# A four-layer graph network on one core: first-layer attention on two halves of the partitions, codes loaded behind the edge tables, look-ups two groups ahead

## The reference

```
feat = x @ W1 -> [N, 4 heads, 16]
e = leaky_relu(el[src] + er[dst]);  ee = exp(e - segment_max(e, dst)[dst])
alpha = ee / segment_sum(ee, dst)[dst]
h = elu(segment_sum(feat[src] * alpha, dst) + b1)        # 64 columns
second step: the same on h @ W2, one head, 128 columns
```

## Time and profile before

| | us |
|---|---|
| median of 3 runs | 2458.64 (2457.08 to 2461.86) |
| the profiled execution, its own time | 2458.36 |
| its span, first to last instruction | 2456.6 |
| prep and stage a, to the barrier | 0 to 537 |
| first softmax | 537 to 580 |
| stage b | 580 to 764 |
| stage c | 764 to 1051 |
| all that comes behind | 1051 to 2457 |

### The profile page before, as it was taken

One profiled execution on the slowest core, in us unless ns is written; L12 is line 12 of the kernel. 1 busy time (PEld: TensorE's weight loads), 2 busy tenths in 40 slices (PEclk: granted clock), 3 DMA queues, 4 the chain that ended last, 5 costly groups with the idle time before them and its releaser, 6 DMA issues.

```text
span 2456.6 us, 32122 instructions
## 1 busy us (share of the span) xinstructions
PE 1917.6 (78%) x7888; PEld 1280.3 (52%) x7888; DVE 1718.3 (70%) x6542; ACT 1120.3 (46%) x3061; POOL 1382.8 (56%) x1388
## 2 busy tenths in 40 slices
PE   2998988975877688847756665999995899969883
PEld 2988888864663223236645553666563222235552
DVE  5644444448775876579968986899895566678773
ACT  0322222214665566625535554566664555524332
POOL 5777777730003677700047773477665777727776
PEclk9766666655556788755558886999997555556655
DMA  5655555544224567624449775233531999923340
GB/s 152 191 155 155 155 156 155 155 156 173 105 109 150 171 184 205 183 81 146 151 133 258 212 208 161 93 130 129 166 121 54 335 367 315 305 72 104 127 139 28
DMA packets 272958, 401.94 MB, mean 164 GB/s; under 512 B 98472, under 2 KB 115009, under 8 KB 272645
## 3 DMA queue, kind: packets, MB, share of 16 engines
q1 hardware_dynamic: 215852, 310.35, 38.8%
q0 software_dynamic: 43904, 75.95, 11.7%
q10 hardware_dynamic: 13016, 13.59, 1.6%
HBM read 222.06 MB, written 185.39 MB: 166 GB/s over the span
## 4 chain that ended last, share of the span: by engine, by line
POOL 16%; DVE 13%; issue 11%; ACT 8%; PE 5%; DMA 2%; POOLq 0%; SPq 0%; DVEq 0%; ACTq 0%
POOL ring L667 8%; POOL big L667 4%; POOL out_dram L673 4%; DVE stats L683 3%; ACT outr L729 3%; DVE G L1161 3%; ACT big L1806 2%; DMA ring<-x_t,idx 1%; DVE mv L692 1%; DVE z L1533 1%; DVE z L1876 1%; PE bank L1549 1%; ACT big L1814 1%; PE bank L1545 1%; ACT hT L1792 1%
## 5 line engine op out<-in xcount | busy, mean ns | idle before, releaser
L729 ACT ACTIVATE outr<-z,rn 128x128 f32<-128x128 f32 x784 | 322.7, 483 | 297.1 <-DMA out_dram<-outr,idx 103.7
L667 POOL DMA_INDIRECT ring<-in_x_dram,idx x392 | 379.9, 969 | 137.3 <-issue 118.3
L667 POOL DMA_INDIRECT ring<-x_t,idx x280 | 266.9, 953 | 303.4 <-SPq L303 209.1
L667 POOL DMA_INDIRECT ring<-hidden_e,idx x196 | 195.5, 997 | 309.2 <-DVE idx L1415 251.6
L673 POOL DMA_INDIRECT x_t<-outr,idx x196 | 234.3, 1195 | 160.5 <-ACT outr L729 114.7
L1161 DVE TENSOR_TENSOR_SCAN G<-cont,G,bank 64x512 f32<-64x512 uint8 (+1 forms) x192 | 240.6, 1253 | 35.1 <-PE bank L1239 32.4
L673 POOL DMA_INDIRECT out_dram<-outr,idx x196 | 195.5, 997 | 102.5 <-issue 58.2
L1937 PE MATMUL bank<-DB,z 20*128 20x512 f32 x196 | 201.2, 1128 | 22.8 <-DVE outr L1391 8.1
L1239 PE MATMUL bank<-ident,msg 128*64 128x128 f32 (+1 forms) x588 | 153.2, 415 | 71.4 <-DVE msg L1146 68.5
L1033 DVE BATCH_NORM_STATS2 stats<-ring 128x6 f32<-128x128 f32 x196 | 42.7, 281 | 232.0 <-DMA ring<-in_x_dram,idx 231.8
L1549 PEld LDWEIGHTS bank<-W_s,G 65*128 65x128 f32 (+1 forms) x784 | 165.5, 311 | 65.7 <-issue 63.3
(11 more groups left out here) (384 smaller groups left out, 4548.4 us busy)
## 6 DMA issues: line engine op xcount, KB each, us to landing
hT<-in_x_dram SPq DMA_DIRECT2D x194, 256.0 KB
x_t<-outr SPq DMA_DIRECT2D x98, 256.0 KB
ring<-x_e SPq DMA_DIRECT2D x98, 256.0 KB
x_t<-xload SPq DMA_DIRECT2D x48, 512.0 KB, 3.2
xsrc_e<-ring SPq DMA_DIRECT2D x49, 256.0 KB, 2.8
xd_e<-ring ACTq DMA_DIRECT2D x49, 256.0 KB
ring<-xsrc_e SPq DMA_DIRECT2D x49, 256.0 KB
x_t<-xT SPq DMA_DIRECT2D x49, 256.0 KB
```

The costliest lines, as they stand in the source:

```text
L667: nc.gpsimd.indirect_dma_start(to(c), None, table, bass.IndirectOffsetOnAxis(ap=idx[:, kind, (g + 1) * GT + c:(g + 1) * GT + c + 1].bitcas ...
L729: ins = nc.scalar.activation(to[:, k, :], frm[:, k, :], ACT.Identity, bias=sc[:, k, 1:2], scale=sc[:, k, 0:1])
```

## The change

Stage b runs on two halves of the edges at once. The first 25 groups (`GA`, 12800 edges) lie on partitions 0 to 63, the other 24 (`GB`) on partitions 64 to 127. Step j handles group j and group 25 + j: two multiplies, four turns of 128 columns, one scan on 128 partitions, the elu on 128 partitions, one join, four products with `W2d` (W2x twice on the diagonal, 132 columns), two copies of rows, one copy `own2`, two stores. There are 25 steps in place of 49 groups. The scan of the second half has to start with the sum that the first half leaves where a node's edges cross the border. This carry is made ahead in the softmax: PE turns the unnormalised weights of the first half back (8 turns), DVE keeps those whose destination is the border's (`mal`, two multiplies), PE sums them over the 100 tiles of the first half with 100 accumulating products of 4 x 64, DVE scales by the weight's denominator, and one product puts it on the partitions (`crow`, `cB`).

The other parts: the `idx0` loads move from the front of ACT's queue to behind the edge tables in it; seven DVE instructions of prep (`table`, `iota`, `pcol`, `rc1`, the ones of `cross` and `ecov`) move from its end to where DVE waits for the edge tables; the mask is loaded in halves (64 partitions each) in prep, and whole again in stage c, from ACT's queue at group 6; the look-ups of stage c run two groups further ahead (`LEAD = 3`), its copies two groups further behind, and the five pieces go behind groups 8, 17, 26, 35, 36. The five pieces of stage b go behind steps 3, 7, 11, 15, 19 (`RATES`). A row of `hidden_e` grows from 65 to 66 columns.

```diff
+GA = (NG + 1) // 2
+GB = NG - GA
+TA, EA = GA * GT, GA * GE
+QA = EA // CH
...
+            if half:
+                for n, frm in ((SRC, src), (DST, dst)):
+                    eng.dma_start(idx[:, n, GT:GT + RING * GT], frm[0:RING * GE].rearrange("(c p) -> p c", p=P),
+                                  allow_slow_non_contiguous=True).then_inc(S("idx0"), 16)
...
+            for n in range(2):
+                k = (EA, EP - EA)[n]
+                sp.dma_start(cont[n * HF:(n + 1) * HF, 0:k], cont_d[0, n * EA:n * EA + k].partition_broadcast(HF)) \
+                    .then_inc(S("cont_in"), 16)
...
+            v.wait_ge(S("iotas"), 3)
+            c.do(v.memset(table[:], 0.0))
+            c.do(v.tensor_copy(iota[:], iota_i[:]))
+            c.do(v.tensor_copy(pcol[:], pcol_i[:]))
+            c.do(v.tensor_copy(rc1[:], rc_i[:]))
+            for t in (cross, ecov):
+                c.do(v.memset(t[:, :, CN - 1:CN], 1.0))
+            c.do(v.memset(ecov[:, :, CN - 2:CN - 1], 0.0))
...
+            if spread is None:
+                pe.wait_ge(S("sm_exp"), turn + 1)
+                for r in range(2):
+                    for h in range(nh):
+                        ins = nc.tensor.transpose(bank[7][:, (r * nh + h) * QA:(r * nh + h + 1) * QA],
+                                                  ee[0:QA, h, r * P:(r + 1) * P], ident[0:QA, 0:QA])
+                ins.then_inc(S("half_pe"), 1)
             pe.wait_ge(S("sm_sum"), turn + 1)
             nc.tensor.matmul(bank[6][Q, 0:nh], linkf[Q, :], fs[Q, :, CH - 1], start=True, stop=True)
             nc.tensor.matmul(bank[6][Q, nh:2 * nh], linkb[Q, :], bs_[Q, :, 0], start=True, stop=True) \
                 .then_inc(S("sm_sumcarry"), 1)
+            if spread is None:
+                pe.wait_ge(S("half_dve"), 1)
+                for t in range(TA):
+                    nc.tensor.matmul(bank[4][0:nh, 0:HF], mal[:, t, :], feat[:, t, 0:HF], start=t == 0, stop=t == TA - 1)
             pe.wait_ge(S("sm_alpha"), turn + 1)
+            if spread is None:
+                nc.tensor.matmul(bank[5][0:nh, 0:1], fs[Q, :, 0], ident[Q, QA:QA + 1], start=True, stop=True) \
+                    .then_inc(S("half_pe"), 1)
             for r in range(2):
                 for h in range(nh):
                     ins = nc.tensor.transpose(bank[r][:, h * NQ:(h + 1) * NQ], ee[Q, h, r * P:(r + 1) * P],
                                               ident[Q, 0:NQ])
             ins.then_inc(S("sm_back"), 1)
+            if spread is None:
+                pe.wait_ge(S("half_dve"), 2)
+                nc.tensor.matmul(bank[5][:, 8:9], crow, ones[0:nh, 0:1], start=True, stop=True) \
+                    .then_inc(S("half_pe"), 1)
 
...
+            if spread is None:
+                v.wait_ge(S("half_pe"), 1)
+                for r in range(2):
+                    ins = c.do(v.tensor_tensor(
+                        mal.rearrange("p (q r) h -> p r h q", r=2)[:, r, :, :],
+                        bank[7][:, r * nh * QA:(r + 1) * nh * QA].rearrange("p (h q) -> p h q", h=nh),
+                        spans.rearrange("p (q r) -> p r q", r=2)[:, r:r + 1, :].to_broadcast([P, nh, QA]), ALU.mult))
+                c.hold()
+                v.sem_inc(S("half_dve"), 1)
...
+            if spread is None:
+                v.wait_ge(S("half_pe"), 2)
+                v.wait_ge(S("b_zero"), 2)
+                c.link(v.tensor_copy(carry[0:nh, 0, 0:1], bank[5][0:nh, 0:1]))
+                c.link(v.scalar_tensor_tensor(crow[:, HF:P].rearrange("p (h d) -> p h d", h=nh),
+                                              bank[4][0:nh, 0:HF].rearrange("p (h d) -> p h d", h=nh), carry[0:nh, 0, 0:1],
+                                              ident[0:nh, 0:nh].unsqueeze(2).to_broadcast([nh, nh, HF // nh]), ALU.mult,
+                                              ALU.mult))
+                v.sem_inc(S("half_dve"), 1)
...
+        def halves(j):
+            return P if j < GB else HF
+
+        RATES = (3, 7, 11, 15, 19)
+
         def b_vector(v):
...
+            def weighs(j):
+                need(v, "b_tr", j - 1)
+                for n in range(2 if j < GB else 1):
+                    ins = v.tensor_tensor(msg[:, j % 2, :, n * HF:(n + 1) * HF].rearrange("p t (h d) -> p t h d", h=HEADS),
+                                          feat[:, four(n * GA + j), 0:HF].rearrange("p t (h d) -> p t h d", h=HEADS),
+                                          alpha[:, four(n * GA + j), 0:HEADS].unsqueeze(3)
+                                          .to_broadcast([P, GT, HEADS, HF // HEADS]), ALU.mult)
+                ins.then_inc(S("b_msg"), 1)
+
+            def scan(j):
+                s, w = j % 2, halves(j)
+                need(v, "b_tr", j + 1)
+                need(v, "b_scan", j)
+                need(v, "b_exp", j - 1)
+                ini = G[0:w, 1 - s, GE - 1:GE] if j else cB
+                v.tensor_tensor_scan(G[0:w, s, :], cont[0:w, j * GE:(j + 1) * GE], bank[s][0:w, :], ini, ALU.mult, ALU.add) \
+                    .then_inc(S("b_scan"), 1)
+
+            def join(j):
+                s, w = j % 2, halves(j)
+                need(v, "b_mm", j - 1)
+                need(v, "b_exp", j + 1)
+                v.scalar_tensor_tensor(hT[0:w, s, 2, :], hT[0:w, s, 1, :], -1.0, hT[0:w, s, 0, :],
                                        ALU.add, ALU.add).then_inc(S("b_h"), 1)
             edge = rates_vector(v, 3, "e", ecov, est, alpha3, est, etemps)
-            pipeline(v, [(-1, weighing(v, "b", feat, HF, HEADS)), (2, join), (0, scanning(v, "b", HF))],
-                     [edge[0], map_table(v), edge[1], rows_of_biases(v), edge[2]])
+            extra = dict(zip(RATES, [edge[0], map_table(v), edge[1], rows_of_biases(v), edge[2]]))
+            c = Chain(v)
+            weighs(0)
+            v.wait_ge(S("half_pe"), 3)
+            c.link(v.tensor_copy(cB, bank[5][:, 8:9]))
+            for j in range(GA + 2):
+                if j + 1 < GA:
+                    weighs(j + 1)
+                if j >= 2:
+                    join(j - 2)
+                if j < GA:
+                    scan(j)
+                if j in extra:
+                    extra[j]()
...
+            def turn(j):
+                s, w = j % 2, halves(j)
+                need(pe, "b_msg", j + 1)
+                need(pe, "b_scan", j - 1)
                 for c in range(GT):
-                    ins = nc.tensor.matmul(bank[2 + s][:, c * (HF + 2):(c + 1) * (HF + 2)],
-                                           hT[0:HF, s, 2, c * P:(c + 1) * P], W2x[:], start=True, stop=True)
+                    ins = nc.tensor.transpose(bank[s][0:w, c * P:(c + 1) * P], msg[:, s, c, 0:w], ident[:])
+                ins.then_inc(S("b_tr"), 1)
+
+            def project(j):
+                s, w = j % 2, halves(j)
+                if j == 0:
+                    pe.wait_ge(S("b_w2"), 32)
+                need(pe, "b_h", j + 1)
+                need(pe, "b_row", j - 1)
+                n = HW * w // HF
+                for c in range(GT):
+                    ins = nc.tensor.matmul(b_rows(j, c // 2)[:, (c % 2) * 2 * HW:(c % 2) * 2 * HW + n],
+                                           hT[0:w, s, 2, c * P:(c + 1) * P], W2d[0:w, 0:n], start=True, stop=True)
                 ins.then_inc(S("b_mm"), 1)
...
-            pipeline(pe, [(0, turning(pe, "b", HF)), (2, project)], [prefix, skip, skip, skip, skip])
+            for j in range(GA + 2):
+                if j < GA:
+                    turn(j)
+                if j >= 2:
+                    project(j - 2)
+                if j == RATES[0]:
+                    prefix()
+
+        def b_rows(j, n):
+            return bank[((2, 3), (4, 7))[j % 2][n]]
...
+            def rows(j):
+                s, n = j % 2, 2 if j < GB else 1
+                need(a, "b_mm", j + 1)
+                if j >= 2:
+                    for k in range(n):
+                        wait(a, f"b_out{2 * s + k}", 16 * (j // 2))
+                to = outf[:, 2 * s:2 * s + n, 0:GT * HW].rearrange("p a (t f) -> p a t f", f=HW)
+                for k in range(2):
+                    ps = b_rows(j, k)[:, 0:4 * HW].rearrange("p (t a f) -> p a t f", t=2, f=HW)
+                    ins = nc.scalar.activation(to[:, :, 2 * k:2 * k + 2, :], ps[:, 0:n], ACT.Copy)
+                ins.then_inc(S("b_row"), 1)
+                need(a, "b_row", j + 1)
+                nc.scalar.activation(own2[:, 0:n, j * GT:(j + 1) * GT], to[:, :, :, HF + 1], ACT.Copy)
...
-            pipeline(a, [(0, split), (2, rows)], [root[0], skip, root[1], skip, root[2]])
+            extra = {RATES[0]: root[0], RATES[2]: root[1], RATES[4]: root[2]}
+            for j in range(GA + 2):
+                if j < GA:
+                    split(j)
+                if j >= 2:
+                    rows(j - 2)
+                if j in extra:
+                    extra[j]()
...
+            for j in range(GA):
+                need(sp, "b_row", j + 1)
```

(50 more changed lines are left out.)

94 lines of the change are left out of this document (35 added, 59 removed).

## The result

The changed kernel takes **2382.75 us** (median of 4 runs, 2379.06 to 2384.5) against 2457.98 of the kernel before beside it: ratio 0.9687, 95% interval 0.9672 to 0.9703. The profiled execution has a span of 2382.7 us where the one before had 2456.6: 73.9 less. Forecast were 2388 and -70.8. The sum is close, but three of its four terms are not, and the fourth, stage b, is right for another reason than the one given.

The account below looks back on a forecast made before the run. Bounds taken: POOL in stages a and c, DVE in the first softmax, PE in stage b. -2.2 + 15.2 - 67.4 - 16.4 = -70.8 against 2458.36 gave 2387.6, with 0.3 added 2388 us; range 2370 to 2408.

Parts of the forecast that it names:

- The softmax, +15.2: First softmax: 200 product records take 28 us ahead of PE's turn back (+14.9), second multiply 0.35; ends +10.7 to +34.8.
- the price of a record, 0.14: First softmax: each of the border chain's 200 PE records costs 0.14 us, 28 us in all.
- rival 1: First softmax: chain of products hidden at 0.066 us a record, only 1.5 us of growth left, 2374; chance 0.12.
- The lower end, 0.117: First softmax: cheapest price taken for a record, half of 0.2375 us; products take 23.4 us, giving +10.7.
- Stage b, -67.4: Stage b: 183.4 us becomes 116.0, PE staying the bound with 25 rounds of 2.92 and pieces 31.1.
- an end of the range: Stage b: PE granted its fast clock, ACT setting the pace at 2.60 a round, -8 from the forecast term.
- Stage c, -16.4: Stage c: POOL's waits for DVE's indices go, 15.7 us, and the first gather comes 0.7 earlier.
- the four-slot ring: Stage c: covers the 3.2 MB mask load at group 6 beside 178 GB/s of other traffic.
- without that cover: Stage c: the mask's load at group 6 would cost about 8 us if the four-slot ring did not cover it.
- The 0.7 from `shifted(0)`: Start of stage c: first gather 0.7 us earlier, since `shifted(0)` is no longer ahead of `hid(0)`.
- Prep and stage a, -2.2: Prep and stage a: first gather at 20.1, 33rd at 60.7 if its slot is free, else 61.1; ends -6 to +6.5.
- Behind stage c, 0: After stage c's last gather: the later stages only shift, with no change in their length.

Follow-up runs that it names:

- the changed-over run: Changed kernel with the border's 100 products' operands swapped (64 weight columns, 4 moving), plus two in old order; chain start to stage b's first multiply 25.17 us against 16.94.

## Why the prediction was right, and where it was not

**The softmax, +15.2: wrong, and the largest miss.** The mis-sized term is the price of a record, 0.14. It is 0.11 at the lower clock and 0.055 at the higher, 0.069 on the mean, so in the softmax rival 1 (0.066, chance 0.12) was what happened: 200 records in 13.8 us under DVE's division, and a softmax longer by 0.5. The lower end, 0.117, was about the price at the lower clock, and I took more. At that clock all the way the 200 records would have taken 21.4 us (the 0.107 of the changed-over run) and ended at 585.7, 7.2 behind DVE. So the price accounts for about half of the miss and the clock for the other half. Against the rival I held the clock of 0.50 in the softmax before; PE did almost nothing there, and with the chain in place it rose. The Trainium skill (TensorE: Matmul & The Clock Gate, "Wait — 56ns, not 53.3ns?") gives about 62 ns per matmul only for decoding in software, a condition that the prediction left out; at 0.055 a record the trace is below that, so it was not the bound of this chain.

**Stage b, -67.4: right in its sum (-68.1), not in its parts.** That the sum came out is luck. I had 25 rounds of PE at 2.92 and five stops of PE, 31.1 together. The experiments show rounds of DVE at 2.44, and so the pieces count with DVE's whole time: the five rounds that hold one take 51.3 us, 39.1 more than five of 2.44, and the round behind each is 0.7 longer. 25 x 0.48 = 12.0 less for the rounds, and 8.0 + 3.6 more for pieces and their followers. The ground was DVE's 2.50 beside PE's 2.92: with less than half a microsecond between them I should have asked which clock PE has once its work is halved in length; the fast clock stood in the prediction, but only as an end of the range, and with ACT as the next to set the pace at 2.60. PE at 1.17 and 0.60 needs 1.77, and at the lower clock it needed 2.77, not 2.92.

**Stage c, -16.4: the mechanism held, the size did not (-9.5, and -0.1 at the start).** The six waits for the indices are gone. What came in their place was named and costed at nothing: the load of the mask, "its cover is the four-slot ring". The ring covers the gathers, not a store that ACT waits for ahead of a root that DVE waits for. Moving the load gives 3.9 back, cutting the pieces 3.4, both 6.1, which ends at the 254 us of the forecast. So the load cost about half of what "without that cover" (8 us) had named. The 0.7 from `shifted(0)` did not show (8.58 against 8.64 from SP's first transfer to the first gather).

**Prep and stage a, -2.2: not there (+0.3).** The first gather came at 20.88 (20.1 forecast), but the first 32 took 1.30 us each, not 1.27 (1.26 to 1.30 in the ten experiments with the codes behind), so the 33rd started at 62.51 rather than 60.7; with the codes behind, POOL's own 32 gathers set that start, and no longer the slot alone. With the codes first the 33rd starts at 60.27. (The row of bandwidth reads 18 to 27 GB/s from 5.5 us on, not 21 to 27; the sum does not hang on it.)

**Behind stage c, 0: +3.0 in this trace, within the spread of the stretch.** In eight experiments, whose instructions there are those of the changed kernel, it takes 1413.8 to 1419.2. Of the kernel before there is one trace (1414.3), so a small cost of the change is not ruled out.

So 2388 was near by luck: 14.7 us less than forecast in the softmax and 0.7 less in stage b were met by 2.5 more in stage a, 6.9 more in stage c and 3.0 more behind it.

## What to carry to other kernels

Take the price of a record from rows that have its weight and its moving columns, and at both clocks, and look which engine's busy time it would lie under before it is added to the path. Where a stage's engine is relieved, compare the next one at the clock that the first will then have; whatever sets the new pace pays for every piece of work put between the rounds in full. A transfer that is moved beside other traffic costs through the waits for stores: follow it to the engine that waits for the store's slot, and to whatever waits for that engine.

## What the runs showed of the hardware

- The same 100 products, with PE busy throughout: with 4 columns of weights and 64 moving the granted clock rose from 0.50 to 1.00 some 5 us in; with 64 and 4 it stayed at 0.50 for 21 us.
- A record of 4 weight columns and 64 moving costs 0.055 us at clock 1.00 and 0.11 at 0.50, one of 64 and 4 the same 0.107 at 0.50, one of 128 and 4 0.214 there, and those with 128 weight columns and 66 moving 0.2375. The price follows the larger side in these rows, not the sum and not the weights alone.
- A broadcast load of 3.2 MB held the DMA at a share of 0.93 to 0.98 for 18 us. The gathers of the stage took 1004 ns on the mean, 997 before; ACT waited 6.42 us for a store's slot, and moving the load to group 21 shortened the stage by 3.9 us.
